# Two mixtures of experts and an attention layer: the first mixture computed for chosen (token, expert) pairs in expert tiles of 512 slots

## The chip, the cores and the metric

One core of one Trainium2 chip runs the whole program. The metric is device time in microseconds (us), the median of the runs. An execution of the kernel before takes 1566.62 us (two runs, 1565.79 to 1567.45).

## What is computed

There are 32 rows of 128 tokens, 128 numbers each. Four blocks follow one another, each adding its output, times the tanh of a gain, to x:

```python
# 1: first mixture. The context routes, 8 experts, 2 chosen, hidden size 512, biases
combine = softmax(top_2(ctx @ Wg + bg))            # zero for the 6 experts not chosen
h = relu(ln(x) @ W1[e] + b1[e]);  y = h @ W2[e] + b2[e]
x = x + tanh(g_xattn[0]) * sum_e combine[e] * y[e]
# 2: second mixture. x itself routes, 4 experts, 2 chosen, gated
h = silu(ln(x) @ w1[e]) * (ln(x) @ w3[e])
x = x + tanh(g_ffn[0]) * sum_e gates[e] * (h @ w2[e])
# 3: attention of the 128 tokens of a row to the 128 context vectors of the same row, 16 heads of 8
x = x + tanh(g_xattn[1]) * attention(ln(x), ctx, mask)
# 4: a gated MLP 128 -> 352 -> 128 whose inputs and weights are rounded blockwise to FP4
x = x + tanh(g_ffn[1]) * fp4_mlp(ln(x))
```

## The kernel before

The 32 rows are cut into 8 groups of 4 rows (`TG = 4`, 512 tokens). Matrices of the mixtures are kept in two halves, "hi" (rounded to fp32r) and "lo" (the rest), and `product` (L875) makes each product of three matmuls: hi with hi, lo with hi, hi with lo. A hidden size of 512 is four chunks of 128 (`FC`).

**First mixture (E0).** All 8 experts are computed for all tokens, so a group has 32 chunks. A chunk is `up` (three matmuls into a bank U, L955), a relu on ACT (L609), the rounding to hi on POOL (L508), the subtraction for lo on DVE (L743), and `down` (three matmuls into a bank Y, L983), which stands three chunks later (`LAG`). After four chunks `combine` multiplies Y by the gate of its expert on DVE (L755) and POOL adds it to `acc` (L515). The gate is spread over the partitions by four transposes (`cbc`, L941).

**Second mixture (E1).** Again all experts for all tokens, 16 chunks a group. A chunk is two products of three matmuls (`w1` and `w3`) over three U banks used in turn, silu on ACT (L614), a multiplication on DVE (L739), hi on ACT (L619), lo on DVE (L743), three matmuls of `down` in turn with L877 to L881.

**Attention and MLP.** Row by row: `s` (scores, L1034), scale and maximum (DVE, L838, L841), `exp` (ACT, L648), `rinv` (DVE, L844), the norm (POOL, L549), `pt` (transposes, L1041), the copy `pT` (ACT, L653), `pv` (L1051), four times for the heads of a row; around it `a_q`, `a_k`, `a_v` and `wo`; then the MLP (`f_*`), whose quantising goes to and fro between DVE and POOL (L679 to L691, L480 to L491).

**The order.** One list of steps, from `expert_order` and `attention_order`, is walked by every engine, and each engine takes its part of every step, in that order. The list of an iteration holds E0 and E1 of group g, and between them, in places counted in "halves" (two a chunk; the table `AT`, a row every 14), attention and MLP of group g-1. So an iteration has two stages: the E0 stage, from the step `("back", 1)` of the group before to `("back", 0)`, and the E1 stage, to the next `("back", 1)`. Both `back` steps end with an addition on DVE (L767). The first mixture's router and layer norm for the next group (`ctxT`, `logits`, `ln`, `lnx`, `xnT`) stand in the E1 stage. Iterations 1 to 6 are one loop on the device with semaphore targets worked out in registers; iterations 0, 7 and the last (attention alone, table `AT_LAST`) are written out.

**Waits that matter.** A `down` waits for its lo. An `up` of E0 waits for the relu two chunks earlier (two U banks). Attention uses two banks M in turn.

## Time and profile before

| what | us |
|---|---|
| median of the two runs | 1566.62 |
| the two runs | 1567.45 and 1565.79 |
| span of the profiled execution, first to last instruction | 1567.5 |
| PE busy in it | 1337.5 |
| DVE busy in it | 1011.9 |
| ACT busy in it | 872.6 |
| POOL busy in it | 716.2 |

Busy time of PE counts an instruction until its modelled end, so rows of pipelined matmuls overlap: the distance between two starts says what a matmul costs, not its duration. A group in the list by line has the number of its instructions, their busy time, the mean duration of one in ns, and the idle time of the engine ahead of them. "PEclk" is the TensorE clock granted, as a share of full speed.

### The profile page before, as it was taken

What the parts mean: (1) busy time and instruction counts of PE and PEld (TensorE: products, weight loads), DVE (VectorE), ACT (ScalarE), POOL (GpSimd) and SP (SyncE); (2) the same over time, 40 slices, a digit from 0 to 9 for tenths busy, and PEclk for the clock granted to TensorE, in tenths of its full rate; (3) what the DMA queues carried; (4) which work ended last, traced back from release to release, by engine and by line L of the source; (5) the groups of instructions that cost most, each with busy time, mean ns of one, the idle gap of its engine ahead of it and who ended that gap; (6) DMA issues with size and microseconds to landing.
All of it is one profiled execution on the core that took longest, in us unless ns stands there. A gap on an engine that the chain in (4) does not pass through costs nothing.

```text
span 1567.5 us, 25069 instructions
## 1 busy us (share of the span) xinstructions
PE 1337.5 (85%) x6350; PEld 979.1 (62%) x6350; DVE 1011.9 (65%) x2377; ACT 872.6 (56%) x2421; POOL 716.2 (46%) x971
## 2 busy tenths in 40 slices
PE   7778988889978898879888899888998898896884
PEld 5556766667656766557666676666666576574552
DVE  6866675856668476766758566585666857574442
ACT  5535764556744575447655466455664477553652
POOL 3533554435534355444634355344553446442342
PEclk9979997999989899999989899799997999996765
DMA  3310000000000000000000000000000000000000
GB/s 99 108 41 4 5 9 15 4 6 7 5 14 4 7 8 6 16 6 8 4 20 2 9 4 10 14 4 8 8 6 14 5 9 5 6 3 7 4 4 4
DMA packets 34084, 20.48 MB, mean 13 GB/s; under 512 B 3624, under 2 KB 31888, under 8 KB 33936
## 3 DMA queue, kind: packets, MB, share of 16 engines
q1 hardware_dynamic: 33936, 18.81, 4.2%
q8 instruction: 56, 0.92, 0.3%
q14 instruction: 92, 0.75, 0.2%
HBM read 16.70 MB, written 2.10 MB: 12 GB/s over the span
## 4 chain that ended last, share of the span: by engine, by line
PE 45%; DVE 20%; issue 15%; POOL 10%; ACT 8%; DVEq 1%; POOLq 0%; SPq 0%; DMA 0%; ACTq 0%
PE M L1034 5%; PE U L1051 5%; PE U L877 4%; DVE h_lo L743 4%; PE U L881 4%; PE U L878 4%; PE Y L877 3%; ACT big L648 3%; PE Y L881 3%; PE M L1021 3%; DVE h L739 3%; PE Y L878 2%; PE M L1041 2%; PE M L1065 2%; POOL big L549 2%
## 5 line engine op out<-in xcount | busy, mean ns | idle before, releaser
L743 DVE TENSOR_TENSOR h_lo<-h,h_hi 128x512 fp32r<-128x512 f32 x384 | 316.9, 828 | 72.6 <-POOL h_hi L508 60.0
L508 POOL TENSOR_SCALAR h_hi<-h 128x512 fp32r<-128x512 f32 x256 | 180.5, 707 | 257.7 <-ACT h L609 230.0
L648 ACT ACTIVATE big<-big,nmax 128x128 f32<-128x128 f32 x512 | 199.8, 395 | 88.8 <-DVE nmax L841 88.3
L609 ACT ACTIVATE h<-U,biasT 128x512 f32<-128x512 f32 x256 | 175.9, 687 | 102.5 <-PE U L881 88.9
L549 POOL TENSOR_TENSOR big<-big,rinv 128x512 f32<-128x512 f32 x128 | 150.3, 1174 | 151.7 <-DVE rinv L844 151.7
L1051 PE MATMUL U<-big,Vr 128*128 128x512 f32 x256 | 150.9, 674 | 24.0 <-ACT big L653 24.0
L1034 PEld LDWEIGHTS M<-kT,qT 8*128 8x128 f32 x944 | 116.1, 189 | 84.3 <-issue 69.6
L1034 PE MATMUL M<-kT,qT 8*128 8x128 f32 x944 | 138.7, 286 | 2.2 <-ACT sg L666 2.1
L877 PE MATMUL U<-xn_hi,w_hi 128*128 128x512 f32 x256 | 119.3, 466 | 21.9 <-DVE h L739 12.9
L844 DVE RECIPROCAL rinv<-rsum 128x4 f32<-128x4 f32 x128 | 22.7, 177 | 174.4 <-ACT big L648 174.4
L619 ACT ACTIVATE h_hi<-h 128x512 fp32r<-128x512 f32 x128 | 80.9, 632 | 84.6 <-DVE h L739 81.7
L877 PE MATMUL U<-xn_hi,W_hi 128*128 128x512 f32 x256 | 121.3, 474 | 4.9 <-DVE h L739 4.6
L877 PE MATMUL Y<-h_hi,W_hi 128*128 128x512 f32 x256 | 116.6, 455 | 0.0
L881 PE MATMUL Y<-h_lo,W_hi 128*128 128x512 f32 x256 | 104.4, 408 | 13.6 <-DVE h_lo L743 13.6
L653 ACT ACTIVATE big<-M 128x512 f32<-128x512 f32 x119 | 70.4, 592 | 73.8 <-PE M L1041 73.6
L515 POOL TENSOR_TENSOR acc<-acc,part 128x512 f32<-128x512 f32 x64 | 87.4, 1365 | 51.0 <-DVE part L755 26.8
L881 PE MATMUL U<-xn_lo,w_hi 128*128 128x512 f32 x256 | 107.3, 419 | 0.0
L878 PE MATMUL U<-xn_hi,w_lo 128*128 128x512 f32 x256 | 106.9, 418 | 0.0
L881 PE MATMUL U<-xn_lo,W_hi 128*128 128x512 f32 x256 | 104.2, 407 | 0.0
L878 PE MATMUL U<-xn_hi,W_lo 128*128 128x512 f32 x256 | 104.0, 406 | 0.0
L878 PE MATMUL Y<-h_hi,W_lo 128*128 128x512 f32 x256 | 101.8, 398 | 0.0
L614 ACT ACTIVATE h<-U 128x512 f32<-128x512 f32 x128 | 76.5, 598 | 44.0 <-PE U L881 35.3
(210 smaller groups left out, 3023.9 us busy)
## 6 DMA issues: line engine op xcount, KB each, us to landing
big<-in_L_xattn_W SPq DMA_DIRECT2D x16, 256.0 KB, 3.0
big<-in_L_ffn_w SPq DMA_DIRECT2D x12, 256.0 KB, 2.8
xin<-in_x SPq DMA_DIRECT2D x8, 256.0 KB, 2.7
nat<-in_ctx SPq DMA_DIRECT2D x8, 256.0 KB, 3.2
ctx<-in_ctx SPq DMA_DIRECT2D x32, 64.0 KB, 1.8
mask_sb<-in_mask_BxSxS_if SPq DMA_DIRECT2D x32, 64.0 KB, 1.9
out_dram<-xatt SPq DMA_DIRECT2D x32, 64.0 KB, 1.6
big<-in_L_ffn_w_down SPq DMA_DIRECT2D x1, 176.0 KB
```

The lines of the kernel that those rows point to most:

```text
L508: nc.gpsimd.tensor_scalar(h_hi[i % 4][:, :], h32[i % 3][:, :], 1.0, 0.0, ALU.mult, ALU.add).then_inc(hi_done, 1)
L515: nc.gpsimd.tensor_tensor(acc[:, :], acc[:, :], part[:, :], ALU.add).then_inc(acc_added, 1)
L549: nc.gpsimd.tensor_tensor(p, p, rinv[:, i % 2, :].unsqueeze(2).broadcast_to([P, HB, S]), ALU.mult).then_inc(norm_done, 1)
L609: nc.scalar.activation(h32[i % 3][:, :], U[i % 2][:, :], ACT.Relu, bias=biasT[:, i:i + 1]).then_inc(relu_done, 1)
L619: nc.scalar.activation(h_hi[i % 4][:, :], h32[i % 3][:, :], ACT.Copy).then_inc(hi_done, 1)
L648: done = nc.scalar.activation(p, p, ACT.Exp, bias=nmax[:, u % 2, r:r + 1], accum_out=rsum[:, u % 2, r:r + 1])
L743: nc.vector.tensor_tensor(h_lo[i % 4][:, :], h32[i % 3][:, :], h_hi[i % 4][:, :].bitcast(fp32), ALU.subtract).then_inc(lo_done, 1)
L877: nc.tensor.matmul(dst, w_hi, x_hi, start=start, stop=False)
L878: nc.tensor.matmul(dst, w_lo, x_hi, start=False, stop=False)
L881: return nc.tensor.matmul(dst, w_hi, x_lo, start=False, stop=stop)
L1034: ins = nc.tensor.matmul(bank[:, c], qT[j % 2][rows, c], kT[j % 2][rows, c], start=True, stop=True)
L1051: ins = nc.tensor.matmul(OA[:, :], Vr[:, r, :], pT[i % 2], start=(r == 0), stop=(r == HB - 1))
```

## The change

The first mixture leaves the iteration and is computed first, for all rows, only for chosen pairs; the rest becomes one unrolled pipeline. `E0` keeps 8 experts with `K0 = 2` chosen. All names below are of the changed kernel.

- **Front.** All context and all x are loaded. PE transposes the context and makes the logits of all rows; x is normalised (statistics on DVE, a power and 32 multiplications of 128x128 on POOL). A chain of some thirty small DVE operations and two matmuls finds for each pair its rank in its expert and from it a slot; each expert starts at a multiple of 512 slots. 23 tiles of 512 slots (`NTILE`) are always computed, whatever the routing; 8192 pairs fill 16. SP fills the 23 tiles of `xs_dram` with zeros (6 MB). The weights are split into hi and lo and stored to DRAM, 1 MB for each expert.
- **Scatter.** POOL issues 64 indirect DMAs (32 rows, 2 choices), each of 128 tokens of 512 bytes, into `xs_dram`.
- **Tiles.** For each tile SP reads the number of its expert and fetches weights (1 MB), biases and inputs. PE turns the inputs (4 transposes), makes 4 chunks `up` and `down` as E0 before (3 chunks of lag, two U banks, two Y banks), and turns the outputs back (4 transposes); relu on ACT, hi on POOL, lo on DVE as before; output rows are stored. Nothing of attention or of E1 lies beside it.
- **Pipeline.** For each group POOL issues 8 indirect DMAs that gather the outputs, DVE mixes them into x by their gates (`mix`). E1, attention and MLP stand in one list over all 32 rows, sorted by a place in units: a row every 14 units (`PER`), with the same offsets as `AT`, but the MLP of each row 29 units after its start; an E1 chunk every 3.5 units, its group's first chunk 70 units ahead of its first row. There is no E0 work in it.
- **Inside E1.** silu is made as a tanh on ACT and one more DVE operation, `(tanh + 1) * gate`; the factor 0.5 is in the gain. The gate product always goes to U0 and waits for that operation on the chunk before (`gated_done`), the other always to U1. lo is made on POOL, not on DVE. The MLP's silu is changed in the same way. Y is one bank, and attention, `cbc`, `xnT`, `logits` and `back` share four M banks in turn.

```diff
-N0, N1 = E0 * FC, E1 * FC
+K0 = 2
+N1 = E1 * FC
+NTILE = (K0 * B * S + E0 * (NT - 1)) // NT
+PER = 14
+ROW_AT = {"a_ln": -3, "a_lnx": -1, "a_cx": 0, "a_q": 1, "a_k": 2, "cap": 2, "a_v": 8,
+          "s": (4, 7, 11, 14), "exp": (1, 1, 2, 2), "rsum": 2, "pt": 5, "pv": 7, "ot": 21, "wo": 25,
+          "f_start": 29, "f_ln": 0, "f_x": (1, 2, 3, 4), "f_xt": 5, "f_g": 6, "f_u": 6,
+          "f_h": (6, 7, 8, 9), "f_ht": 13, "f_dn": 15}
+MOE_AT = {"first": -70, "cbc": 0.5, "up": 0, "swiglu": 1, "lo": 2, "down": 4, "combine": 4.2, "back": 6.5}
+PREP_AT = {"gather": -50, "mix": -26, "ln": -24, "lnx": -20, "xnT": -14, "logits": -9}
...
 # SP
+            for i in range(NTILE):
+                sp.dma_start(xs_dram[i * NT:(i + 1) * NT, :].rearrange("(j p) d -> p j d", p=P), Vr[:, :, :]).then_inc(xs_zeroed, 16)
...
+                e = sp.value_load(owni[0:1, i:i + 1], min_val=0, max_val=E0 - 1)
+                sp.dma_start(wt[i % 3][:, :].bitcast(fp32), w_dram[bass.ds(e, 1)].rearrange("a p n -> p (a n)")).then_inc(wt_loaded[i % 3], 16)
...
 # POOL
+            pool.wait_ge(normed, 1)
+            pool.wait_ge(slots_made, 1)
+            pool.wait_ge(xs_zeroed, 16 * NTILE)
+            for b in range(B):
+                for c in range(K0):
+                    nc.gpsimd.indirect_dma_start(xs_dram, bass.IndirectOffsetOnAxis(ap=slot[:, c, b:b + 1], axis=0),
+                                                 xall[:, b, :], None).then_inc(scattered, 16)
...
+                if what == "gather":
...
+                    for j in range(TG):
+                        for c in range(K0):
+                            nc.gpsimd.indirect_dma_start(yg[:, j, c, :], None, ys_dram,
+                                                         bass.IndirectOffsetOnAxis(ap=slot[:, c, i * TG + j:i * TG + j + 1], axis=0)).then_inc(gathered, 16)
...
+                elif what == "lo":
+                    pool.wait_ge(hi_done, i + 1)
+                    nc.gpsimd.tensor_tensor(h_lo[i % 4][:, :], h32[i % 3][:, :], h_hi[i % 4][:, :].bitcast(fp32), ALU.subtract).then_inc(lo_done, 1)
...
 # DVE
+                elif what == "swiglu":
+                    dve.wait_ge(tanh_done, i + 1)
+                    nc.vector.scalar_tensor_tensor(h32[i % 3][:, :], h32[i % 3][:, :], 1.0, U[0][:, :], ALU.add, ALU.mult).then_inc(gated_done, 1)
+                    dve.wait_ge(gated_done, i + 1)
+                    dve.wait_ge(upf_done, i + 1)
+                    nc.vector.tensor_tensor(h32[i % 3][:, :], U[1][:, :], h32[i % 3][:, :], ALU.mult).then_inc(swiglu_done, 1)
...
 # PE, tiles
+            for n, i, c in tile_chunks():
+                if c == 0 and i + 1 < NTILE:
+                    xs_turn(i + 1)
...
+                    product(U[n % 2][:, :], w[:, 0:F][:, cs], w[:, F:2 * F][:, cs], xn_hi[i % 2][:, :], xn_lo[i % 2][:, :]).then_inc(up0_done, 1)
+                if LAG0 <= n < NCH + LAG0:
+                    down0(n - LAG0)
...
 # PE, pipeline
+                elif what == "up":
...
+                    if i >= 1:
+                        pe.wait_ge(gated_done, i)
+                    product(U[0][:, :], w1_hi[:, e, c], w1_lo[:, e, c], xn_hi[g % 2][:, :], xn_lo[g % 2][:, :]).then_inc(gate_done, 1)
+                    if i >= 1:
+                        pe.wait_ge(swiglu_done, i)
+                    product(U[1][:, :], w3_hi[:, e, c], w3_lo[:, e, c], xn_hi[g % 2][:, :], xn_lo[g % 2][:, :]).then_inc(upf_done, 1)
```

The order of PE's instructions before, in the E0 stage of an iteration (U, Y are the mixture's banks, M and the L1051 output the attention's):

```order
L952 REGISTER_ALU
L877 MATMUL U<-xn_hi,W_hi 128x512
L878 MATMUL U<-xn_hi,W_lo 128x512
L881 MATMUL U<-xn_lo,W_hi 128x512
L927 REGISTER_ALU
L1051 MATMUL U<-big,Vr 128x512
L1034 MATMUL M<-kT,qT 128x128 x4
L975 REGISTER_ALU
L877 MATMUL Y<-h_hi,W_hi 128x512
L878 MATMUL Y<-h_hi,W_lo 128x512
L881 MATMUL Y<-h_lo,W_hi 128x512
```

PE now, in the pipeline, where attention is densest (OA is the attention output's bank):

```order
L990 MATMUL U<-xn_hi,w_hi 128x512
L991 MATMUL U<-xn_hi,w_lo 128x512
L994 MATMUL U<-xn_lo,w_hi 128x512
L1190 MATMUL M<-wgT,xqT 128x352
L1190 MATMUL M<-wuT,xqT 128x352
L1179 MATMUL OA<-big,Vr 128x512
L1165 MATMUL M<-kT,qT 128x128 x4
L990 MATMUL Y<-h_hi,w_hi 128x512
L991 MATMUL Y<-h_hi,w_lo 128x512
L994 MATMUL Y<-h_lo,w_hi 128x512
L1157 MATMUL M<-WvT,cxT 128x128
L1171 MATMUL M<-ident,big 128x128 x4
```

The products between two pieces of attention were E0's (W); they are E1's (w) now, and MLP matmuls (L1190) stand among the scores of another row.

POOL before, in the E0 stage (h_hi is the rounding of E0's chunks, big the norm of the attention):

```order
L508 TENSOR_SCALAR h_hi<-h_0 128x512
L547 REGISTER_ALU
L549 TENSOR_TENSOR big<-big,rinv 128x512
L504 REGISTER_ALU
L506 REGISTER_ALU
L508 TENSOR_SCALAR h_hi<-h_1 128x512
```

POOL now, in the pipeline, at a gather:

```order
L526 TENSOR_TENSOR h_lo<-h_1,h_hi 128x512
L519 DMA yg<-ys_dram,slot 128x128 x8
L561 TENSOR_TENSOR big<-big,rinv 128x512
L499 TENSOR_TENSOR qv<-hh,q_rcp 128x352
L526 TENSOR_TENSOR h_lo<-h_2,h_hi 128x512
L561 TENSOR_TENSOR big<-big,rinv 128x512
L503 TENSOR_TENSOR qv<-qv,qm 128x352
L505 TENSOR_TENSOR qv<-qv,qm 128x352
L507 TENSOR_TENSOR hh<-qv,q_scale 128x352
```

E1's lo stands on POOL between the norms, and once a group eight DMA issues stand ahead of a norm.

## Rows read from the trace of the kernel before

**Rows 1.** The page: busy time by engine, the span in 40 slices

```profile
PE 1337.5 (85%) x6350; PEld 979.1 (62%) x6350; DVE 1011.9 (65%) x2377; ACT 872.6 (56%) x2421; POOL 716.2 (46%) x971
...
PEclk9979997999989899999989899799997999996765
DMA  3310000000000000000000000000000000000000
GB/s 99 108 41 4 5 9 15 4 6 7 5 14 4 7 8 6 16 6 8 4 20 2 9 4 10 14 4 8 8 6 14 5 9 5 6 3 7 4 4 4
```

**Rows 2.** Timeline of DVE, the additions that end stages: start us, us, instruction

```profile
254.77 0.74 DVE L767 SCALAR_TENSOR_TENSOR x<-Z,tg,xin 128x512 f32<-128x512 f32 x1
...
326.36 0.75 DVE L767 SCALAR_TENSOR_TENSOR xmid<-Z,tg,x 128x512 f32<-128x512 f32 x1
...
440.08 0.74 DVE L767 SCALAR_TENSOR_TENSOR x<-Z,tg,xin 128x512 f32<-128x512 f32 x1
...
1426.89 0.75 DVE L767 SCALAR_TENSOR_TENSOR xmid<-Z,tg,x 128x512 f32<-128x512 f32 x1 [1.27 <-PE Z L988]
```

**Rows 3.** Windows: length us, busy us of PE, PEld, DVE, ACT, POOL; PEclk, DMA, GB/s

```profile
20.00:60.00 40.00, 37.61 (x166) 29.29 (x164) 29.99 (x41) 25.05 (x42) 24.25 (x28) 1.00 0.27 79
...
150.00:254.00 104.00, 97.22 (x519) 71.68 (x518) 67.73 (x129) 69.96 (x224) 56.00 (x67) 1.00 0.02 7
254.00:337.00 83.00, 67.08 (x292) 49.48 (x291) 57.66 (x165) 37.03 (x76) 33.17 (x54) 0.90 0.04 10
...
1427.00:1567.00 140.00, 98.79 (x377) 66.63 (x375) 54.37 (x150) 65.22 (x222) 43.24 (x64) 0.65 0.02 5
```

**Rows 4.** Timeline of PE in an E0 stage: start us, us, instruction

```profile
163.01 0.48 PE L877 MATMUL U<-xn_hi,W_hi 128*128 128x512 f32 x1
163.32 0.39 PE L878 MATMUL U<-xn_hi,W_lo 128*128 128x512 f32 x1
163.55 0.40 PE L881 MATMUL U<-xn_lo,W_hi 128*128 128x512 f32 x1
...
164.49 1.02 PE L1051 MATMUL U<-big,Vr 128*128 128x512 f32 x2
165.44 1.15 PE L1034 MATMUL M<-kT,qT 8*128 8x128 f32 x8
166.52 0.50 PE L877 MATMUL U<-xn_hi,W_hi 128*128 128x512 f32 x1
```

**Rows 5.** Timeline of PE, gates of E0 in iteration 0: first and last of five

```profile
28.23 0.60 PE L941 MATMUL Z<-ident,gates 128*128 128x128 f32 x4
...
55.73 0.49 PE L941 MATMUL Z<-ident,gates 128*128 128x128 f32 x3
```

**Rows 6.** Groups by line: count, busy us, mean ns, idle before

```profile
L743 DVE TENSOR_TENSOR h_lo<-h,h_hi 128x512 fp32r<-128x512 f32 x384 | 316.9, 828 | 72.6 <-POOL h_hi L508 60.0 <-issue 11.5 <-DVE xmid L767 0.2
...
L508 POOL TENSOR_SCALAR h_hi<-h 128x512 fp32r<-128x512 f32 x256 | 180.5, 707 | 257.7 <-ACT h L609 230.0 <-PE Y L881 24.3
L609 ACT ACTIVATE h<-U,biasT 128x512 f32<-128x512 f32 x256 | 175.9, 687 | 102.5 <-PE U L881 88.9 <-DVE h_lo L743 10.4
...
L549 POOL TENSOR_TENSOR big<-big,rinv 128x512 f32<-128x512 f32 x128 | 150.3, 1174 | 151.7 <-DVE rinv L844 151.7
...
L739 DVE TENSOR_TENSOR h<-U,h 128x512 f32<-128x512 f32 x128 | 87.5, 684 | 1.6 <-DVE xatt L850 1.2 <-PE U L881 0.4
...
L614 ACT ACTIVATE h<-U 128x512 f32<-128x512 f32 x128 | 76.5, 598 | 44.0 <-PE U L881 35.3 <-DVE h_lo L743 6.0
...
L648 ACT ACT_TABLE_LOAD x18 | 23.1, 1283 | 0.3
```

**Rows 7.** DMAs: an issue on SP's queue (timeline), landing of 64 KB (by line)

```profile
4.42 0.43 SPq L413 DMA_DIRECT2D bg_bc<-in_L_xattn_bg  x1
...
ctx<-in_ctx SPq DMA_DIRECT2D x32, 64.0 KB, 1.8
```

More of the change, by code:

```diff
@@ new lines, with pipeline_order, put @@
+M_STEPS = {"a_cx", "a_q", "a_k", "a_v", "s", "pt", "wo", "f_xt", "f_g", "f_u", "f_ht", "f_dn",
+           "cbc", "xnT", "logits", "back"}
+LN_STEPS = {"a_ln", "f_ln"}
+def pipeline_order():
+    timed = []
+    def put(t, *step):
+        timed.append((t, len(timed), step))
+    for g in range(NG):
+        t0, gap = MOE_AT["first"] + PER * TG * g, PER / TG
+        for what, t in PREP_AT.items():
+            put(t0 + t, what, g)
+        for n in range(N1):
+            q, t = g * N1 + n, t0 + gap * n
+            if n % FC == FC - 1:
+                put(t + MOE_AT["cbc"], "cbc", q // FC)
+            for what in ("up", "swiglu", "lo", "down"):
+                put(t + MOE_AT[what], what, q)
+            if n % FC == FC - 1:
+                put(t + MOE_AT["combine"], "combine", q // FC)
+        put(t0 + gap * (N1 - 1) + MOE_AT["back"], "back", g)
+    for b in range(B):
+        t0, at = PER * b, ROW_AT
+        for what in ("a_ln", "a_lnx", "a_cx", "a_q", "a_k", "a_v", "cap", "ot", "wo"):
+            put(t0 + at[what], what, b)
+        for r, first in enumerate(at["s"]):
+            u = b * HB + r
+            put(t0 + first, "s", u)
+            for h, later in enumerate(at["exp"]):
+                put(t0 + first + later, "exp", u * HB + h)
+            for what in ("rsum", "pt", "pv"):
+                put(t0 + first + at[what], what, u)
+        tf = t0 + at["f_start"]
+        for what in ("f_ln", "f_x", "f_xt", "f_g", "f_u", "f_h", "f_ht", "f_dn"):
+            for part, h in enumerate(at[what] if what in ("f_x", "f_h") else (at[what],)):
+                put(tf + h, what, b * QPARTS + part if what in ("f_x", "f_h") else b)
+    order = [step for _, _, step in sorted(timed)]
+    check_order(order)
+    return order
@@ L672, in _ @@
-            each_iteration(act, walk)
+                if 6 <= k < 2 * E0 and k % 2 == 0:
+                    act.wait_ge(w_stored, 16 * (k // 2 - 2))
+                nc.scalar.activation(pieces[k][1], stage[k % 4][:, :], ACT.Copy).then_inc(wsplit_hi, 1)
+            for k in range(4):
+                split_hi(k)
+            act.wait_ge(gdA_made, 1)
+            nc.scalar.activation(gtA[:, :], gdA[:, :], ACT.Tanh, scale=0.5).then_inc(gtA_made, 1)
+            act.wait_ge(l1w_turned, 1)
+            for c, dst in ((0, WqT), (1, WkT)):
+                nc.scalar.activation(dst[:, :, :].rearrange("p i (j r) -> p (i j) r", r=32)[:, :, 0:DK],
+                                     M[0][:, c * P:(c + 1) * P].rearrange("p (h d) -> p h d", d=DK), ACT.Copy)
@@ L675, in _, with link, split_lo @@
         @block.vector
         def _(dve):
-            def quantise(part, t, q, link):
+            steps = [0]
+            def link(ins):
+                steps[0] += 1
+                ins.then_inc(dve_step, 1)
+                dve.wait_ge(dve_step, steps[0])
+            def split_lo(k):
+                dve.wait_ge(wsplit_hi, k + 1)
+                _, hi, lo = pieces[k]
+                nc.vector.tensor_tensor(lo, stage[k % 4][:, :], hi.bitcast(fp32), ALU.subtract).then_inc(wsplit, 1)
+            for dst in (WqT, WkT, Vr):
+                nc.vector.memset(dst[:, :, :], 0.0)
@@ new lines, in _ @@
+            picks = ohs[:, :, :].rearrange("p b e -> p (b e)")
+            nc.tensor.matmul(Y[:, 0:B * E0], before[:, :], picks, start=True, stop=True)
+            nc.tensor.matmul(Y[:, B * E0:2 * B * E0], all_ones[:, :], picks, start=True, stop=True).then_inc(ranks_made, 1)
+            pe.wait_ge(l1w_loaded, 16 * 17)
+            for w in range(4):
+                ins = nc.tensor.transpose(M[0][:, w * P:(w + 1) * P], attw_nat[:, w, :], ident[:, :])
+            ins.then_inc(l1w_turned, 1)
```

1502 lines of the change are left out of this document (766 added, 736 removed).

## The prediction
> **What bounds the kernel now.** I read the page first. PE is busy 85% of the span, DVE 65%, ACT 56%, POOL 46%, at nearly full clock up to the last 140 us [rows 1]. PE is nearest to its limit, but busy time counts pipelined matmuls to their modelled ends, so I took starts: three matmuls of a product stand 0.23 us apart [rows 4], so an E0 chunk (six) costs PE 1.40 us and an E1 chunk (nine) 2.10 us. In the same rows one `pv` costs 0.95 us and one `s` 1.08 us; with `pt` 0.36 (its distance in the same timeline) a fourth of a row's attention is 2.4 us, and with q, k, v, wo and the MLP's matmuls (some 4.7 us) a row is 14.3 us.
>
> An iteration then asks PE for 32 x 1.40 = 44.8 (E0), 16 x 2.10 = 33.6 (E1), 4 x 14.3 = 57.2 (rows), 12 x 0.35 = 4.2 (gates) and about 4.3 of small ones: 144 us. It takes (1426.89 - 326.36) / 6 = 183.4 us [rows 2], 1.27 times PE's work. The two stages differ. The E0 stage takes 440.08 - 326.36 = 113.7 us for about 97.6 us of that work (all E0, the attention of four rows, one MLP): 1.17 times, PE 93% busy in its window, nobody else over 67%. The E1 stage takes 326.36 - 254.77 = 71.6 us for the other 46.4: 1.54 times, with DVE the nearest to PE [rows 2, 3]. So E0 is easy work: it fills PE and asks little of the others. What stays behind is the hard part. The run ends with attention alone, 140 us for four rows [rows 3].
>
> **The change part by part.**
>
> *What goes.* 256 chunks of E0 are 358 us of PE; 92 come back (23 tiles of four) with 129 us. So PE saves 230 us, less than the rule "two of eight" suggests, since seven tiles are padding at least. But the 358 us lay beside attention, and the 129 us now lie alone.
>
> *Front, up to the scatter.* At the start DMA moves 99 to 108 GB/s at a share of 0.3 [rows 1], so some 330 GB/s at its fullest. Context, x, first pieces, layer-1 weights and 6 MB of zeros are 12 MB: 37 us, and SP issues over 60 DMAs at 0.43 to 0.5 us [rows 7], 30 us beside it. Statistics, POOL's 32 multiplications and DVE's thirty small operations come to about 40 us. The zeros end last. I take 48 us (38 to 65).
>
> *Scatter.* 64 indirect DMAs on POOL, in a row, with PE idle. The trace has none. From below: an issue on SP's queue, 0.43 us [rows 7]; from above: the whole way of 64 KB from issue to landing, 1.8 us [rows 7]. I take the middle, 1.1 us: 70 us (28 to 115). Then landing, first input, its transposes and splits: 7 us. The weights' splitting and storing go on behind it.
>
> The Trainium skill ("DMA: Bandwidth & Descriptors", section Anatomy of one DMA) gives a DMA issued from GpSimd 2.0 us and its bytes at 436 GB/s. One after another that would be 2.15 us each, 138 us for the scatter and a sum 67 us higher; no run here shows it yet, and the page itself puts most of the 2 us into the receipt, which issues behind it need not wait for. The sum goes by my 1.1.
>
> *Tiles.* Iteration 0 shows E0 without attention: five gates from 28.23 to 55.73, four experts in 27.5 us, 6.9 us for four chunks [rows 5], where PE's work is 5.95. DVE is busy 30.0 of 40 us there [rows 3], for each expert four lo (0.83, [rows 6]), two weight splits and a combine. A tile has four lo, one input lo, one copy and in the first twelve one split, about as much, and four more transposes. 23 x 6.9 = 159 us (145 to 185).
>
> *Between tiles and pipeline.* The last tile's outputs drain and are stored, eight gathers (8 x 1.1), mix, layer norm, transposes and split follow, all serial: 28 us (20 to 40). PE's clock falls there; it is back soon in dense work.
>
> *Lead of E1.* 70 units, 20 chunks, without attention. U0 is now one bank with a loop: product 0.70, its end 0.17, tanh 0.60 (the size of L614), DVE 0.68 (L739) and three handings over of about 0.1: 2.5 us against 2.10 of PE [rows 6]. 52 us.
>
> *The mixed part.* E1 ends 378 units after row 0 starts, so 27 rows have E1 beside them. A row with its four chunks asks PE for 8.4 + 14.3 + 0.9 = 23.6 us. DVE: its 1011.9 less all lo (384, 317 us) and about 100 for E0's combines, router, norms and splits, plus 128 x 0.68 for the new operation, plus 43 for mix and the MLP's: 725 / 32 = 22.6. POOL: 716.2 less 180.5 of hi and about 96 for additions, norms and router, plus 128 lo at 1.17 (L549, also two inputs in SBUF), plus 64 gathers at 1.1: 660 / 32 = 20.6. ACT: 872.6 less 176 relus and about 117 for gates, setup and table loads: 18.1 [rows 1, 6]. Three engines within 15% of one another, in order, each waiting for the others. The factor before was 1.27; 23.6 x 1.27 = 30.0. Table loads go (37 of 1.28 us, of which the 18 at L648 are shown [rows 6]; ACT loads one table now) and so do registers before waits: I take off 0.6, so 29.4 us a row, 27 x 29.4 = 794 us.
>
> *Gathers on POOL.* Eight issues stand in one piece ahead of a norm: 8.8 us. Behind them wait the norm, lo and the quantising; PE needs the norm three units (6.3 us) later. I charge 3 us for each of seven groups, 21 us.
>
> *Tail.* Attention alone from the last E1 on: five rows. Four take 140.6 us now [rows 2, 3]; a fifth adds an estimated 21. 161 us.
>
> *Sum.* 48 + 70 + 7 + 159 + 28 + 52 + 794 + 21 + 161 = 1340 us, against a span of 1567.5, which is within 1 us of the median of the runs: 227 us less.
>
> *Edits costed at nothing.* Weight fetches: 1 MB a tile and about 0.75 MB beside it, 5.3 us at 330 GB/s under a tile of 6.9 us, asked for 1.4 tiles ahead; uncovered they are the fourth rival. One Y bank: its `combine` stands right behind the last `down`, 3.5 units ahead of the next. Four M banks for all: a fill has four steps to be emptied, against two before.
>
> **The rivals.**
>
> *A: the hard part stays hard.* Without E0 as filler the mixed part behaves as the E1 stage does, 1.54 times PE's work, or 1.37 without the 8 us or so that its serial start takes; halfway, 1.45, gives 34.2 us a row and 1340 + 27 x 4.8 = 1470 us. For it: DVE and POOL now carry about as much as PE, and the U0 loop is tighter. Against it: the serial start is pulled ahead and attention is spread evenly.
>
> *B: the pipeline is as good as the E0 stage.* 1.17 times: 27.6 us a row, less the gather charge: 1340 - 49 - 21 = 1270 us. For it: the same offsets ran so, with slack of 7 units where the attention's chain needs 8 us. Against: nobody but PE was over 67% there.
>
> *C: slower than before.* POOL pays for each indirect DMA with its own time, and much more than I think: at two landings each, 3.6 us. 64 in the scatter, 8 at the start of the pipeline and 56 in clumps ahead of norms are 128 times 2.5 us more: 320 us, so 1660 us. It decides from 3.1 us an issue (1340 + 128 x 2.0 = 1596). For it: nothing of it is in the trace, and lo on DVE ran 828 ns on average where the same operation with POOL idle takes some 690, so the two engines do disturb one another [rows 6]. Against: it is twice the way of 64 KB. The Trainium skill ("SBUF — State Buffer", the box on the DVE blocking DMA) says that GpSimd can't write descriptors while DVE holds their shared port, and sets 620 ns alone against 3100 ns beside a copy on DVE. By that rule the scatter, beside quantising and splitting on DVE, and the gathers would be this rival; nothing here bears on it so far but the stretched lo.
>
> *D: the tiles wait for weights,* so that the change doesn't do what it says. At 150 GB/s, 1.75 MB a tile take 11.7 us: 23 x 4.8 = 110 more, 1450 us. Against: 330 GB/s by the share shown, and three buffers.
>
> **How the numbers follow.** Forecast 0.56 (own range 1290 to 1400: a row between 28 and 31 us and the bounds of the scatter), A 0.20, B 0.14, C 0.06, D 0.04. The predicted time is the forecast's, 1340 us. For 8 in 10 the range reaches to B and to A: 1250 to 1470. A measurement of this kernel can tell about 2% from no change, so the border is at 1535 and 1598. Forecast, A, B and D are all under it except for A's far end; C is above it but for its low end: faster 0.92, within 2% 0.03, slower 0.05.
>
> **What would show it.** In the profile of the changed kernel: the first L990 product at about 125 us; the last tile at about 285; the first L1165 (scores) near 370; `back` additions (L927) 4 x 29.4 = 118 us apart; the last 161 us with PE at a low clock. Idle time of PE in the mixed part should be spread over DVE, ACT and POOL. A tile longer than 8 us speaks for D; distances of 137 us between `back` steps for A, of 110 for B. An issue of L478 over 3 us, or L561 waiting long behind L519, is C. I'm wrong if the scatter or the mixed part misses its range, and above all if the time is over 1535 us.

## The result and the profile after

The changed kernel takes 1649.11 us (median of two runs, 1649.09 to 1649.12) against 1566.62 us before: a ratio of 1.053, with an interval of 1.050 to 1.056. It is slower by 82 us, where 227 us less was forecast. The profiled execution has a span of 1647.4 us.

The page of the changed kernel, in the form of [rows 1]: busy time, the granted clock and DMA in 40 slices of 41 us, and the shares of the chain that ended last.

```profile
PE 1173.2 (71%) x5232; PEld 837.9 (51%) x5232; DVE 889.7 (54%) x2197; ACT 694.9 (42%) x2190; POOL 767.5 (47%) x981
...
PEclk9999999968878888889888988888898898886765
DMA  9584766400000000000000000000000000000000
...
PE 35%; DVE 24%; POOL 11%; issue 11%; ACT 10%; SPq 5%; DMA 5%; DVEq 0%; POOLq 0%; ACTq 0%
```

The work went as meant: PE is busy 164 us less and DVE 122 us. No engine is near its limit any more, the chain is shared by PE, DVE, POOL and ACT, and the granted clock in the loop has fallen from mostly 9 to mostly 8.

The same kernel in stages, in the columns of [rows 3]: up to the first scatter, to the first tile product, the tiles, the gap, the lead, the mixed part, the tail.

```profile
0.00:56.00 56.00, 22.34 (x103) 21.06 (x103) 29.69 (x172) 9.90 (x24) 34.65 (x46) 1.00 0.82 220
56.00:150.00 94.00, 5.04 (x18) 3.22 (x19) 22.64 (x53) 9.62 (x17) 64.21 (x67) 1.00 0.66 228
150.00:324.00 174.00, 154.52 (x728) 122.59 (x727) 98.04 (x149) 96.09 (x149) 57.70 (x92) 1.00 0.61 197
324.00:349.00 25.00, 3.25 (x15) 2.91 (x15) 5.33 (x21) 0.60 (x1) 8.99 (x10) 0.52 0.14 42
349.00:431.00 82.00, 58.76 (x208) 41.08 (x209) 39.24 (x100) 24.38 (x44) 37.39 (x41) 0.81 0.04 10
431.00:1469.00 1038.00, 801.63 (x3691) 562.05 (x3690) 613.92 (x1489) 484.49 (x1686) 500.58 (x631) 0.86 0.04 10
1469.00:1647.00 178.00, 127.63 (x475) 85.03 (x473) 80.80 (x217) 69.83 (x269) 63.96 (x95) 0.67 0.02 5
```

Beside the terms of the forecast (us):

| term | forecast | measured | off by |
|---|---|---|---|
| up to the scatter | 48 | 56.0 | +8 |
| 64 scatters | 70 | 82.7 | +13 |
| landing to first tile product | 7 | 11 | +4 |
| 23 tiles | 159 | 174 | +15 |
| gap | 28 | 25.6 | -2 |
| lead of E1 | 52 | 81.6 | +30 |
| mixed part with its gathers | 815 | 1037.7 | +223 |
| tail | 161 | 178.7 | +18 |
| sum | 1340 | 1647.4 | +307 |

The three rows of instructions from which the table's borders come (lines with their count, duration, first and last start):

```profile
L478 POOL DMA_INDIRECT xs_dram<-xall,slot x64: 954/958/1464, 56.0 to 137.7; - x64
L990 PE MATMUL U<-xn_hi,wt x92: 392/398/768, 149.7 to 317.5; 128*128 128x512 f32 x92
L927 DVE SCALAR_TENSOR_TENSOR xmid<-M,tg,xin x8: 741/750/752, 425.6 to 1468.7; 128x512 f32<-128x512 f32 x8
```

L927 is what L767 (xmid) was in [rows 2]. Before, the first of these eight stood at 144.3 us in the trace and the last at 1426.9, 183.2 us for a group of four rows. Now the first stands at 425.6 and the seven steps take 1043.1 us, 149.0 each. So the difference adds up in three terms: 281.3 us more ahead of the first group, 7 x 34.2 = 239.5 less in the loop, 38.1 more in the tail, 79.9 us. The change pays about 280 us up front for taking E0 out of the loop and gets 240 back, where the forecast's rows promised 7 x (183.4 - 117.6) = 461.

Who waited for whom from 560 to 1400 us (us in total, times, longest):

```profile
ACT h_hi L655 <- DVE h L909: 326.1, 87, 6.4
...
DVE rinv L958 <- ACT big L679: 153.2, 56, 4.1
...
PE U L990 <- DVE h L906: 61.8, 45, 2.1
PE M L1187 <- POOL xnf L507: 52.0, 21, 5.4
PE M L1171 <- POOL big L561: 35.3, 10, 6.6
```

The first row is what the forecast had no term for. ACT stands 326 of 840 us ahead of the copy to h_hi, waiting for DVE's second gating multiplication. `exp` (L679) stands behind that copy in ACT's list, and DVE's reciprocal (L958) waits for `exp`: DVE and ACT hold one another. Before, the same wait (h_hi L619 for L739) was 62 us in the 987 us from 440 to 1427.

What one such wait does to PE, in its timeline from 569.79 us (the gather clump of eight issues stands on POOL there, ahead of a norm):

```profile
570.66 0.40 PE L991 MATMUL Y<-h_hi,w_lo 128*128 128x512 f32 x1
570.90 0.40 PE L994 MATMUL Y<-h_lo,w_hi 128*128 128x512 f32 x1
571.13 0.39 PE L1157 MATMUL M<-WvT,cxT 128*128 128x128 f32 x2
577.90 1.09 PE L1171 MATMUL M<-ident,big 128*128 128x128 f32 x4 [6.38 <-POOL big L561]
578.63 0.78 PE L990 MATMUL U<-xn_hi,w_hi 128*128 128x512 f32 x1
579.21 0.63 PE L991 MATMUL U<-xn_hi,w_lo 128*128 128x512 f32 x1
579.63 0.63 PE L994 MATMUL U<-xn_lo,w_hi 128*128 128x512 f32 x1
580.06 0.63 PE L990 MATMUL U<-xn_hi,w_hi 128*128 128x512 f32 x1
580.49 0.58 PE L991 MATMUL U<-xn_hi,w_lo 128*128 128x512 f32 x1
580.90 0.39 PE L994 MATMUL U<-xn_lo,w_hi 128*128 128x512 f32 x1
581.13 0.40 PE L990 MATMUL Y<-h_hi,w_hi 128*128 128x512 f32 x1
```

Read the distances of the starts. Ahead of the wait and from 580.90 on they are 0.23 to 0.24 us; behind it, from 579.21 to 580.49, 0.43 us: the lower of TensorE's two clock levels, 1.2 for 2.4 GHz. The wait of 6.4 us costs about one more in the matmuls behind it (five distances of 0.41 to 0.58 us that are 0.23 at the full clock). So four causes could make a mixed row 38.4 us (1037.7 / 27) where 29.4 was forecast: the loop over U0, POOL's share, the low clock, and offsets in the common list that are too tight.

### The profile page after: what moved, and what is told of

It is laid out like the page before. It is cut to its first block, busy times and chain, and to the rows that moved or that the text cites. A ratio compares the mean times of both kernels' runs of the same rounds, so it can differ in the third digit from the quotient of the medians.

```text
span 1647.4 us, 18117 instructions
## 1 busy us (share of the span) xinstructions
PE 1173.2 (71%) x5232; PEld 837.9 (51%) x5232; DVE 889.7 (54%) x2197; ACT 694.9 (42%) x2190; POOL 767.5 (47%) x981
## 4 chain that ended last, share of the span: by engine, by line
PE 35%; DVE 24%; POOL 11%; issue 11%; ACT 10%; SPq 5%; DMA 5%; DVEq 0%; POOLq 0%; ACTq 0%
PE M L1165 7%; PE OA L1179 5%; DVE big L952 4%; DVE h L906 4%; PE U L990 4%; POOL yg L519 4%; PE U L994 3%; PE U L991 3%; DVE h L909 3%; ACT big L679 3%; POOL h_lo L526 3%; PE M L1190 2%; ACT h_hi L655 2%; DVE nmax L955 2%; PE Y L994 2%
## 5 line engine op out<-in xcount | busy, mean ns | idle before, releaser
L526 POOL TENSOR_TENSOR h_lo<-h,h_hi 128x512 fp32r<-128x512 f32 x128 | 164.9, 1289 | 172.7 <-ACT h_hi L655 172.7
L561 POOL TENSOR_TENSOR big<-big,rinv 128x512 f32<-128x512 f32 x128 | 133.4, 1042 | 170.1 <-DVE rinv L958 170.0
L679 ACT ACTIVATE big<-big,nmax 128x128 f32<-128x128 f32 x512 | 198.5, 392 | 16.9 <-DVE nmax L955 16.9
L1179 PE MATMUL OA<-big,Vr 128*128 128x512 f32 x256 | 154.4, 689 | 13.9 <-ACT big L684 13.9
L952 DVE SCALAR_TENSOR_TENSOR big<-M,cap 128x512 f32<-128x512 f32 x128 | 88.3, 690 | 106.8 <-PE M L1165 105.8
L958 DVE RECIPROCAL rinv<-rsum 128x4 f32<-128x4 f32 x128 | 22.8, 178 | 221.2 <-ACT big L679 219.1
L1171 PE MATMUL M<-ident,big 128*128 128x128 f32 x512 | 89.6, 303 | 35.7 <-POOL big L561 35.7
L492 POOL TENSOR_SCALAR h_hi<-h 128x512 fp32r<-128x512 f32 x92 | 57.7, 627 | 122.5 <-ACT h L621 122.5
L821 DVE TENSOR_TENSOR h_lo<-h,h_hi 128x512 fp32r<-128x512 f32 x92 | 63.7, 693 | 74.2 <-POOL h_hi L492 69.7
L679 ACT ACTIVATION_READ_ACCUMULATOR big<-big,nmax 128x1 f32 x512 | 98.0, 191 | 0.0
L906 DVE SCALAR_TENSOR_TENSOR h<-h,U 128x512 f32<-128x512 f32 x128 | 86.2, 674 | 17.3 <-ACT h L649 17.3
L909 DVE TENSOR_TENSOR h<-U,h 128x512 f32<-128x512 f32 x128 | 88.5, 692 | 4.4
L955 DVE TENSOR_REDUCE nmax<-big 128x4 f32<-128x512 f32 x128 | 87.8, 686 | 4.4
```

The lines of the kernel that those rows point to most:

```text
L526: nc.gpsimd.tensor_tensor(h_lo[i % 4][:, :], h32[i % 3][:, :], h_hi[i % 4][:, :].bitcast(fp32), ALU.subtract).then_inc(lo_done, 1)
L561: nc.gpsimd.tensor_tensor(p, p, rinv[:, i % 2, :].unsqueeze(2).broadcast_to([P, HB, S]), ALU.mult).then_inc(norm_done, 1)
L679: done = nc.scalar.activation(p, p, ACT.Exp, bias=nmax[:, u % 2, r:r + 1], accum_out=rsum[:, u % 2, r:r + 1])
L906: nc.vector.scalar_tensor_tensor(h32[i % 3][:, :], h32[i % 3][:, :], 1.0, U[0][:, :], ALU.add, ALU.mult).then_inc(gated_done, 1)
L909: nc.vector.tensor_tensor(h32[i % 3][:, :], U[1][:, :], h32[i % 3][:, :], ALU.mult).then_inc(swiglu_done, 1)
L952: nc.vector.scalar_tensor_tensor(p, bank[:, :].rearrange("p (h k) -> p h k", h=HB), DK ** -0.5, cap[:, :].unsqueeze(1).broadcast_to([P, HB ...
```

## The experiments

Every run is compared with 1649 us for the changed kernel; the kernel before, taken again beside them, had medians of 1565 to 1572 us and single executions of 1559 to 1575 us. All but e15 and e18 (four executions each) were executed once. Single runs of the same stretch of code differ by some us: the last back step of e8, e12 and e18, whose code is the same up to there, stood at 1320.8, 1326.6 and 1328.3 us. So nothing under 10 us is read from a single run, and a difference of 12 us is only just above that.

**e1: was E0 a filler?** The kernel before, with E0's columns taken away and everything else kept.

```diff
-product(U[i % 2][:, :], W1_hi[:, e, c], W1_lo[:, e, c], xn_hi[0][:, :], xn_lo[0][:, :])
+product(U[i % 2][:, 0:16], W1_hi[:, e, c], W1_lo[:, e, c], xn_hi[0][:, 0:16], xn_lo[0][:, 0:16])
```
and the same for E0's relu, hi, lo, down, combine and additions.

> The kernel before, with the first mixture's chunk operations on all engines cut from 512 columns to 16 (most of the first mixture is left out; number of instructions, order and waits are those of before). It asks what the first mixture's columns cost where they stood beside attention. The forecast's view (PE's work sets a row, at a factor of 1.27): an iteration asks PE for some 105 us in place of 144, 50 us less of 183 in each of seven, so 1220 us, and the stretch between starts of iterations falls to some 133 us. Rival, E0 was filler in waits that attention and E1 have anyway: most of the 183 us stays, 160 to 175 us an iteration, 1450 to 1510 us, with PE's busy share down from 85% to some 65% and its granted clock under 0.9.

Measured: 1642 us, slower than with the whole work. Page and the window of one E0 stage (330 to 448 us):

```profile
PEclk9996566958688666966759566695767956587776
...
330.00:448.00 118.00, 111.64 (x533) 91.28 (x532) 46.85 (x133) 60.62 (x227) 31.78 (x69) 0.66 0.03 7
```

The same stage of the kernel before:

```profile
330.00:438.00 108.00, 98.65 (x516) 73.06 (x515) 68.73 (x132) 71.40 (x226) 57.30 (x69) 0.98 0.02 6
```

An iteration is 198 us long (L771 at 838.10 and 1036.06; 196 on average) where it was 183. DVE, ACT and POOL have 11 to 26 us less to do in the stage; PE's matmuls are as many, 16 columns in place of 512, and its granted clock there is 0.66 in place of 0.98. Over the whole run the `pv` group has a mean of 949 ns for 674, and the stage is longer, 121.7 us (328.7 to 450.4) for 113.7. Both expectations missed. But e1 changes two things at once, the columns and through them the clock: it shows that taking the columns away gives nothing back here, not that they would cost nothing at an equal clock. That was not tried (with filler matmuls in the narrowed stage). How much the loop gives back when E0 leaves it whole, instructions and waits too, the other runs show: 34 us a group in the changed kernel and 51 in e18, where the forecast had 66.

**e2 and e17: the U0 loop.** e2 has three U banks in rotation and three M banks; e17 has three M banks alone.

```diff
-NM = 4
+NM = 3
-if i >= 1: pe.wait_ge(gated_done, i)
-product(U[0][:, :], w1_hi ...
+if i >= 2: pe.wait_ge(swiglu_done, i - 1)
+product(U[2 * i % 3][:, :], w1_hi ...
```

> The changed kernel with three U banks that rotate through gate and up products, and three M banks in place of four. Only the loop over U0 goes. Theory U (the U0 loop holds PE up): PE's waits for L906 (85 us) go, and with them 50 to 80 us: 1570 to 1600 us, back steps 146 us apart. Theory order (every engine works the same list with little slack, so a wait that goes turns up at the next one), theory POOL: under 15 us gained, 1635 to 1650, PE's waits move to the M banks. Three M banks alone could cost 10 us.

> The changed kernel with three M banks in the pipeline and the fourth left idle; U0 and U1 as they are. e2 (three M, three U) took 1687 us. Theory U: the bank costs more than e2 shows, 1715 to 1740 us, so that breaking the U0 loop was worth 30 to 50 us. If the U0 loop costs nothing that another wait doesn't take: 1680 to 1695 us, all of e2's loss is the M bank's.

Measured: 1687 and 1684 us. Waits of PE in the mixed part of e2, then of e17:

```profile
PE M L1154 <- ACT qT L672: 55.6, 24, 3.4
PE U L991 <- DVE h L907: 45.7, 46, 1.3
```

```profile
PE U L991 <- DVE h L907: 91.4, 63, 2.2
PE M L1154 <- ACT qT L672: 61.2, 24, 3.4
```

The bank costs 35 us, and the waits for ACT's q go with it, of which the changed kernel has 15 us, at another step. With three M banks, breaking the U0 loop halves the waits for the gating (91 to 46 us) and gains nothing: they come back elsewhere. Theory U falls, as far as three M banks show it; three U beside four M banks was not tried.

**e3, e4 and e7: POOL.** e3 moves E1's lo to DVE, e4 stands the eight gathers of a group 2.5 units apart, e7 does both.

```diff
-elif what == "lo": (POOL)  nc.gpsimd.tensor_tensor(h_lo ...
+elif what == "lo": (DVE)   nc.vector.tensor_tensor(h_lo ...
-put(t0 + t, "gather", g)
+for k in range(8): put(t0 + t + 2.5 * k, "gather", 8 * g + k)
```

> The changed kernel with the second mixture's lo parts on DVE again, where the kernel before had them, in place of POOL. Theory POOL (POOL's share sets the row): POOL's busy time in the mixed part falls by 108 x 1.29 = 139 us, DVE's grows by 75 to 90 us, L994 no longer waits behind gathers; 1580 to 1610 us. Theory order: DVE is in the chain before every gate product already (L906 behind scores), so its 0.7 us more for each chunk cost as much as POOL's go: 1640 to 1680 us.

> The changed kernel with the eight gathers of a group 2.5 units apart in the order, in place of all at one place. Theory POOL: groups with a clump take 153.6 to 156 us from back to back, the one without 140.0; a clump is 8 x 1.25 = 10 us on POOL. Spread, they hide in POOL's waits and six groups gain some 10 us each: 1580 to 1600 us. Rival, the 14 us are the mix, norms and router of the next group on DVE and PE, not the gathers: 1635 to 1650 us, back steps still over 150 apart.

> Both edits that gained 42 to 45 us alone: lo on DVE and the gathers spread. If they remove different costs (lo's 1.29 us on POOL in the chain of each chunk; the clump of 10 us for a group), the gains add: 1649 - 87 = 1562 us, within 2% of the kernel before. If both only made POOL free at the moments when the gathers stood ahead of lo, they share one gain: 1595 to 1605 us.

Measured: 1604, 1607 and 1590 us. Alone they gain 45 and 42 us, together 59, of 87 if they had added: they partly remove the same waits, POOL work standing ahead of what PE needs. Theory POOL holds, for 59 us. Of e4's 42 us, 32 are in the loop (1043.1 to 1011.4 us from first to last back step) and 11 ahead of it.

**e5: the clock.** Useless matmuls ahead of PE's operand waits.

```diff
+if what in ("s", "pt", "a_q", "a_k", "f_xt", "f_g", "f_ht"):
+    for _ in range(2):
+        nc.tensor.matmul(bank[:, :], w1_hi[:, 0, 0:P], w1_hi[:, 0, :], start=True, stop=True)
```

> The changed kernel with useless matmuls added: two of 128x512 (w1_hi by itself) into the step's own M bank, overwritten by the step, ahead of the operand waits of s, pt, a_q, a_k, f_xt, f_g and f_ht: 26 for a row, 13 for a group of four steps, 0.213 us each at the full clock, 5.5 us a row, 177 us of PE over 32 rows. Theory clock (without E0 the gaps in PE's work lower its granted clock, 0.86 in the mixed part and 0.67 in the tail, and the low clock stretches what PE does between the waits): the clock goes over 0.95, the rest of PE's work in the mixed part shrinks from 800 us to about 690, and the time stays or falls, 1590 to 1650 us, though PE has 177 us more to do. Theory order (the waits alone set the row, the clock is a consequence without a price): the added work lies partly in waits, partly on the chain that PE has 35% of: 1680 to 1750 us.

Measured: 1651 us with 832 more matmuls. Mixed part and tail of e5, and the mixed part of the changed kernel between the same two events (its tail, 178 us at 0.67, stands in the list of stages above):

```profile
424.00:1490.00 1066.00, 909.68 (x4397) 664.68 (x4398) 617.33 (x1493) 487.20 (x1690) 503.87 (x632) 0.93 0.04 10
1490.00:1649.00 159.00, 125.31 (x618) 84.87 (x617) 81.66 (x218) 68.67 (x269) 64.61 (x97) 0.92 0.02 6
```

```profile
425.00:1469.00 1044.00, 806.72 (x3711) 565.44 (x3710) 617.97 (x1494) 486.82 (x1690) 503.60 (x633) 0.86 0.04 10
```

The clock rises, and 177 us of added PE work cost nothing over the whole run: 22 us more in the mixed part, 19 less in the tail. PE's other work shrinks to some 760 us in the mixed part (909.7 less the 27 x 5.5 added), not to the 690 expected. In the tail the low clock has a price: every run without fillers and without the attention's room has a tail of 178.2 to 184.2 us, and e5, with 130 matmuls more, has 159.2. In the mixed part e5 doesn't tell two readings apart: a price that the added work eats up again, or added work that lies in waits and a clock that costs little. By either, lifting the clock doesn't repair the loop.

**e6, e9, e10, e13 and e14: room in the list.** e6 has both parts of this edit, e9 the first, e10 the second; e13 and e14 split the first.

```diff
-MOE_AT = {..., "swiglu": 1, "lo": 2, "down": 4, "combine": 4.2, "back": 6.5}
+MOE_AT = {..., "swiglu": 1, "hi": 2, "lo": 3, "down": 5.5, "combine": 5.7, "back": 7.5}
-elif what == "swiglu": (ACT) nc.scalar.activation(h_hi ...
+elif what == "hi":     (ACT) nc.scalar.activation(h_hi ...
```
```diff
-"rsum": 2, ... "f_xt": 5, "f_g": 6, "f_u": 6, "f_h": (6, 7, 8, 9), "f_ht": 13, "f_dn": 15
+"rsum": 3, ... "f_xt": 7, "f_g": 8, "f_u": 8, "f_h": (8, 9, 10, 11), "f_ht": 15, "f_dn": 17
```
e13 has `"hi": 2, "lo": 2.2` and down, combine and back as they were; e14 has lo at 3, down at 5.5, combine and back later, and the copy where it was.

> The changed kernel with more room between the steps of one chain, instructions and buffers unchanged: E1's copy to h_hi one unit behind swiglu (it stood at swiglu's place in ACT's list), lo at 3, down at 5.5, back at 7.5, rsum 3 behind the scores in place of 2, f_xt to f_dn two units later. Theory order (offsets that were made for 183 us per four rows are too tight where a unit is PE work of 1.7 us): ACT's waits for L909 (326 us in the mixed part) and DVE's for L679 (153 us) fall by half, PE's for L507 (52 us) go: 1560 to 1600 us, back steps 142 apart. Theory POOL: what holds is the amount on POOL and its gather clumps, which stay: over 1635 us.

> The changed kernel with only E1's part of the slack: the h_hi copy a unit behind swiglu in ACT's list, lo at 3, down at 5.5, back at 7.5. e6 gained 94 us with this and the attention's part. If ACT's hold behind swiglu (326 us of waits for L909, exp standing behind it, and DVE's L958 behind exp) is what ties the engines together, this part brings 60 to 80 of the 94: 1570 to 1590 us. If rsum and the MLP were the tight ones: 1625 to 1645 us.

> The changed kernel with only the attention's and the MLP's part of the slack: rsum 3 units behind its scores in place of 2, f_xt to f_dn two units later. By the first reading of e9 this brings 15 to 35 us: 1615 to 1635 us (DVE no longer waits for exp at L958, but exp itself still stands behind L909's result). By the second 60 to 80: 1570 to 1590 us.

> The changed kernel with only ACT's copy to h_hi one unit behind swiglu (lo at 2.2 to stay behind it; down, combine and back as they were). Theory hold (ACT stands 326 us in the mixed part for L909, with exp behind it): ACT's waits for L909 fall under 60 us and 60 to 90 of e9's 101 us are there: 1560 to 1590 us. Theory distance: what counts is lo and down; then the copy, a unit later with down where it was, makes PE wait longer for h_lo (L994), 1640 to 1680 us.

> The changed kernel with lo at 3, down at 5.5, combine at 5.7, back at 7.5, and the copy to h_hi where it was. Theory hold: ACT's waits for L909 stay over 300 us and little is gained, 1625 to 1650 us. Theory distance: 1560 to 1590 us.

| | us | against 1649 |
|---|---|---|
| e6, whole slack | 1555 | -94 |
| e9, E1's part | 1548 | -101 |
| e10, attention's part | 1661 | +12 |
| e13, only the copy later | 1817 | +168 |
| e14, only lo and down later | 1624 | -25 |

E1's part does it all, with the same instructions, buffers and waits. It gained more than I had expected (101 us for 60 to 80), and the attention's part, for which both readings had a gain, cost 12. e6 came out just under its range, with ACT's waits for L909 at 43 us. ACT's wait in e9, and in e14 where the copy stays behind swiglu (430 to 1390 us; the changed kernel has 371.8 in that window):

```profile
ACT h_hi L655 <- DVE h L909: 43.7, 75, 0.8
```

```profile
ACT h_hi L655 <- DVE h L909: 378.6, 90, 9.3
```

But neither half does it alone. PE's longest wait in e13:

```profile
PE Y L994 <- POOL h_lo L526: 121.4, 44, 8.6
```

With the copy a unit later and `down` left where it was, ACT no longer holds (42 us in that window), and PE waits for lo instead: 1205 us from first to last back step in place of 1043. Both ranges for e13 were too low. e14 keeps ACT's wait whole and gains 25 us all the same, so lo and `down` count by themselves; from e14 to e9 only the copy moves, and that is worth 76 us. So the hold of ACT is the larger part, and it can be removed only where `down` is moved too: the hold and the distance from the copy to `down` are one budget. Of its settings, three were tried here (copy, lo, `down` at 2, 2.2, 4; at 1, 3, 5.5; at 2, 3, 5.5) and one beside the other edits (e16).

**e8, e11, e12, e15, e16 and e18: together.** e8 and e18 are e7 with the whole slack; e11 is that with lo on POOL; e12 is e8 with e5's matmuls in the last five rows; e15 is e7 with E1's part alone; e16 is e15 with copy, lo, down, combine and back at 2.3, 3.6, 6.3, 6.6 and 9.

> lo on DVE, gathers spread, and the slack of e6. Theory order: a further 40 to 60 us under e7, 1510 to 1540 us, faster than the kernel before. Theory clock: the slack doesn't fill PE, but with fewer stalls the clock rises too, from 0.86 to over 0.9. If slack is worth nothing, as in e7.

> Gathers spread and the whole slack, lo on POOL as in the changed kernel: e8 without lo on DVE. If lo's place costs by its latency alone (1.29 us in the chain of each chunk), the slack hides it and the two are within 10 us: 1485 to 1495 us, or under 1480, since DVE has 78 us less to do. If POOL's load still counts: 1510 to 1535 us.

> e8 with two useless 128x512 matmuls ahead of the operand waits of s, pt, a_q, a_k, f_xt, f_g and f_ht in the last five rows alone: 130 more matmuls, 28 us at the full clock. Theory clock for the tail (attention alone runs at 0.71 of the clock in e8, and in e5 the tail was 159 us where it was 178): clock over 0.9 there and 10 to 20 us less, 1466 to 1476 us. If e5's shorter tail came from something else (where its last back step stood): 1486 to 1500 us.

> lo on DVE, gathers spread, and the second mixture's slack (e9) without the attention's. If the three add and the attention's part costs here what it cost alone (12 us): 1549 - 59 to 87 = 1462 to 1490 us, as or under e8's 1486, over 5% faster than the kernel before. If the attention's part helps once ACT no longer holds: over 1490 us.

> e15 with the copy at 2.3, lo at 3.6, down at 6.3, combine at 6.6 and back at 9. If the remaining waits of PE for L906 and L994 come of too little room: 10 to 20 us under e15. If e9's slack was enough and a later back only holds the next group up: 0 to 15 us over it.

> The kernel of e8, in rounds. If the attention's slack helps once ACT no longer holds: 1483 to 1489 us and a ratio of 0.948 to the kernel before, clearly under e15's 0.959. If e8 was a lucky look: 1495 to 1505 us.

| | us | ratio to the kernel before |
|---|---|---|
| e8 (single run) | 1486 | |
| e18 (the same, four executions) | 1491.6 | 0.951 (0.946 to 0.956) |
| e11, lo on POOL | 1532 | |
| e12, warm tail | 1488 | |
| e15, without the attention's part | 1500.6 | 0.959 (0.956 to 0.963) |
| e16, still more room | 1546 | |

- The version of e18 is faster than both kernels: 75 us under the one before, 157 us under the changed one. e15 lies 9 us over it. e8 had come out under its range of 1510 to 1540, at a clock of 0.88 and not over 0.9; e18 lies between its two ranges.
- lo on DVE is worth 46 us with the slack (e11 against e8), as much as without it. Slack does not hide it: by e11's expectation that speaks for POOL's load and against lo's latency alone (1.29 us on POOL, 0.71 on DVE).
- e12 gains nothing over the whole run: its tail is 159.6 us at a clock of 0.90, where e8's is 163.1 at 0.71. With the attention's room the tail is short already, and the 19 us of e5 are not there a second time.
- More room is not better without end: e16 is 45 us slower than e15, where 0 to 15 was the worse reading. In e16 PE waits 100.8 us for xnf (L511 there) from 430 to 1390 us, where it waits 71.3 in e15.

The attention's room is two effects that nearly cancel. From first to last back step it costs time, and in the tail it saves time, with ACT's hold and without it:

| | ahead of the first back step | seven groups | tail |
|---|---|---|---|
| changed kernel, and with the attention's part (e10) | 425.6, 426.8 | 1043.1, 1070.4 | 178.7, 162.0 |
| e9, and with it (e6) | 417.3, 416.1 | 948.8, 978.2 | 179.8, 159.0 |
| e15, and with it (e18) | 410.1, 404.1 | 906.4, 924.2 | 181.9, 163.1 |

So e15 has the fastest loop of all runs, 129.5 us a group. That room in the last rows alone would bring it to some 1478 us (410.1 + 906.4 + 161) is an estimate from this table; it was not tried.

Windows of the mixed part and the tail of e18 (the tail's from 4 us ahead of the last back step), then of e15:

```profile
403.00:1324.00 921.00, 774.45 (x3676) 555.68 (x3676) 686.13 (x1594) 492.49 (x1676) 381.38 (x516) 0.87 0.04 11
1324.00:1491.00 167.00, 123.94 (x507) 84.84 (x505) 88.42 (x228) 73.00 (x283) 65.22 (x98) 0.70 0.02 6
...
410.00:1317.00 907.00, 732.85 (x3698) 520.87 (x3697) 674.01 (x1604) 500.50 (x1688) 387.93 (x518) 0.92 0.04 12
1317.00:1498.00 181.00, 131.95 (x480) 87.99 (x478) 80.86 (x217) 69.91 (x269) 64.20 (x95) 0.65 0.02 5
```

A group takes (1328.3 - 404.1) / 7 = 132.0 us in e18, where the changed kernel takes 149.0 and the kernel before 183.2. Still PE has 23.6 x 4 = 94.4 us of work in it: 1.40 times (1.37 in e15, 1.58 in the changed kernel). The factor before was 1.27.

## Why the prediction was wrong

**The mixed part is the term that failed: 223 of 307 us.** What failed is the step from work to time. What a row asks of the engines was close: in the 27 rows DVE, POOL and ACT are busy 22.7, 18.5 and 17.9 us a row, where 22.6, 20.6 and 18.1 were worked out. But the working took the whole loop's factor, 1.27, and put it on what was left. The working itself had found that E0 is easy work and that what stays is the hard part, and rival A was built on it; I gave it 0.20 where it should have been the forecast. A row took 38.4 us, 1.63 times its PE work (1.58 from back step to back step), more than A's 1.45 and than the E1 stage's 1.54.

*What the runs showed in its place.* E1's own list was tighter than before, and that I had not priced. Before, swiglu and the copy to h_hi stood one chunk behind their `up`, and `down` three chunks (`LAG`). In `MOE_AT` they stand 1 unit and 4 units behind it, and a chunk has 3.5 units. At the forecast's 29.4 / 14 = 2.1 us a unit, ACT comes to the copy 2.1 us after the chunk's first matmul; the products, tanh and DVE's two operations need 1.40 + 0.58 + 0.67 + 0.69 = 3.3 us, by estimate from the durations in the traces. So ACT stands, with attention's `exp` behind it. I read the waits for resources (banks, queues, the U0 loop) and looked at no wait that the order makes between ACT and DVE, though the trace of before shows it there already, at 62 us.

Room for the copy and for `down` gives 101 us back (e9), 76 of them by the copy (e9 against e14). With lo and the gathers moved as well (e15) the loop takes 129.5 us a group in place of 149.0, against 117.6 forecast: of the 31.4 us too many a group, 19.5 are these edits', and 11.9 remain in what rival A called the hard part. Their cause was not separated.

**The gather charge** was right in kind. I had 21 us for the mixed part; spreading them gives 32 there and 11 ahead of it (e4). The clump is 8 x 1.25 us, and one holds PE for 6.4 us in the rows above and for 8.9 us in the lead.

**The lead: 30 us too little.** The cycle of 2.6 us a chunk is there: PE's third `down` matmuls stand at 355.18 and 357.78, and at 377.89, 380.49 and 383.25. What I left out is that a gather clump falls into it too, this time ahead of lo:

```profile
PE Y L994 <- POOL h_lo L526: 15.3, 12, 8.9
...
PE U L990 <- DVE h L906: 6.2, 4, 2.0
```

with the matmuls behind it 0.43 us apart again, at a mean clock of 0.81. The charge for gathers started only with the mixed part. It is a third of the miss: with the gathers spread the first back step comes 10.6 us earlier (e4). The other 19 us were not traced to a cause.

**Scatter: the size was off, the rival's side wasn't.** An issue takes POOL 0.958 us (median) and they stand 1.30 us apart (81.7 / 63), where I took 1.1 from the bounds 0.43 and 1.8. Rival C (3.6 us) is excluded: it needed 3.1. The Trainium skill's 2.0 us and more for a DMA issued from GpSimd ("DMA: Bandwidth & Descriptors", Anatomy of one DMA) does not describe the spacing of these, which is 1.25 to 1.30 us. The Trainium skill's stretch of such a DMA from 620 to 3100 ns beside a copy on DVE ("SBUF — State Buffer", A bandwidth-pool intuition that's wrong) was not met, but no DVE copy of that kind stood beside them either. What the trace shows is smaller: 56 of the 64 scatters take 0.95 to 0.96 us, and the eight from 1.03 to 1.46 us all stand beside DVE's quantising or weight splits, as at 68.24 (1.42 us) and 81.32 (1.46 us). The gathers lie between 940 and 1107 ns with DVE busy 59% of the mixed part.

**Tiles: 15 us too little, and not for want of weights.** 7.6 us a tile for 6.9. PE waits there 17.8 us for its inputs from DRAM and never for the weights, so rival D is excluded:

```profile
PE M L1047 <- DMA xatt<-xs_dram: 6.7, 7, 1.0
PE M L1047 <- DMA nat<-xs_dram: 5.6, 6, 1.1
PE M L1047 <- DMA xmid<-xs_dram: 5.5, 6, 1.0
```

These 17.8 us are about the size of the miss, and I had no term for them. SP's list, which waits 95 us for the outputs of earlier tiles (L830) ahead of its later requests, is the likely reason for the late inputs; that was not tested.

**Front and tail.** The front took 56 us, since POOL's 32 multiplications (0.79 us each) end at 55.8, behind the statistics; the zeros are hidden. The tail took 178.7 us for 161, and the 161 was read from a stage with offsets of its own (`AT_LAST`, with `rsum` at 3), while the changed kernel has one table for all rows (`rsum` at 2). With the attention's room it is 159 to 163 us (e6, e8, e10, e18), so the tail's offsets account for it; which of them, was not tried apart. The other way to shorten it is the clock (e5, 159 us).

**What was right:** each engine's work in a row, a tile but for its wait for inputs, the gap, the chunk's cycle in the lead, and that nothing waits for weights. The sign was wrong since what lies ahead of the loop came within 67 us of its price, and the loop gave back 240 us for 461.

**What stays open.** How much of the 1.40 left in e18 is PE's low clock (0.87 in its mixed part), and how much are waits, was not separated. Filler matmuls were tried in the whole pipeline of the changed kernel and in the tail of e8, not in e8's mixed part. Two parts of the change were never undone by themselves: silu as tanh and a second DVE operation (0.67 us in each chunk's chain), and the MLP 29 units after its row's start, beside the scores of other rows. Whether the front could be shortened (POOL's multiplications and scatters, 108 us) was not tried either.

## What to carry to other kernels

Work that fills a busy engine beside a latency-bound chain saves less than its factor of time when it leaves (here 240 us of the 461 counted on), and the part of it that must be done elsewhere, alone, costs its full time: ask what the loop takes without it before counting what it saves. When work leaves an in-order list that several engines share, the distances between its steps must be set again in time, not in places; look for a wait on one engine that another chain's work stands behind (here a copy on ACT right behind its producer, ahead of `exp`), and move the wait and its consumer together: the copy alone cost 168 us, lo and `down` alone gained 25, both gained 101. Look at loop and tail apart too, since one table of distances need not suit both. A factor of busy time to elapsed time belongs to a stage, not to a kernel.
